# Gated delta-rule attention on one core: the carried part of the second tile scaled on GpSimd and summed in PSUM, both key-query products masked in one instruction, and a new order of issue

## The reference, cut to what matters

```python
decay = where(tril, exp(g[:, None] - g[None, :]), 0)
M = where(stril, (k_beta @ k.T) * decay, 0)
T = solve_triangular(eye + M, eye)
v_c, k_cumdecay = T @ v_beta, T @ (k_beta * exp(g)[..., None])
# over the chunks, with a state of 128x128:
v_new = v_i - k_cumdecay @ state
out = (q_i * exp(g_i)[:, None]) @ state + (q_i @ k_i.T * dec_i) @ v_new
state = state * exp(g_last) + (k_i * exp(g_last - g_i)[:, None]).T @ v_new
```

## Time and profile before

| what | value |
|---|---|
| median of three runs | 1482.04 us |
| the profiled execution | 1480.87 us |
| its span in the trace | 1479.0 us |
| granted TensorE clock over the span | 0.974 |
| PE / DVE / ACT / POOL busy, share of the span | 89% / 77% / 68% / 35% |
| rounds of the attention | 64, the first `w` 0 at 81.0 us, the last at 1143.1 us |

### The profile page before, as it was taken

The page is one execution under the profiler, slowest core; times in us unless marked ns, Lnnn a source line. Parts: engine busy times, 40 slices in busy tenths (PEclk is TensorE's granted clock), DMA queues, the critical chain, the costliest instruction groups (busy, mean ns, idle before and its releaser), DMA issues.

```text
span 1479.0 us, 34092 instructions
## 1 busy us (share of the span) xinstructions
PE 1309.4 (89%) x11516; PEld 927.9 (63%) x11516; DVE 1138.0 (77%) x2414; ACT 1002.5 (68%) x2170; POOL 517.4 (35%) x599
## 2 busy tenths in 40 slices
PE   2679999999999999999999999999987559999995
PEld 2247666766667676767667676766665436666664
DVE  4678978889898989888898989898866445555555
ACT  2579788897979798888979797988865212222221
POOL 0134242334334242433333342424323105555550
PEclk9999999999999999999999999999999859999998
DMA  2111010101011010101010110100001016444441
GB/s 82 41 39 52 9 51 9 52 9 58 14 47 44 16 52 9 51 9 52 9 58 27 33 45 16 52 23 16 23 15 33 1 36 182 150 150 152 157 153 39
DMA packets 44659, 76.37 MB, mean 52 GB/s; under 512 B 7172, under 2 KB 26022, under 8 KB 44488
## 3 DMA queue, kind: packets, MB, share of 16 engines
q1 hardware_dynamic: 44488, 74.19, 16.1%
HBM read 72.85 MB, written 1.32 MB: 50 GB/s over the span
## 4 chain that ended last, share of the span: by engine, by line
PE 70%; DVE 16%; issue 7%; ACT 5%; DMA 1%; DVEq 1%; SPq 1%; ACTq 0%
PE bank L563 13%; PE bank L517 9%; PE bank L780 8%; PE bank L733 6%; DVE sil L1132 5%; PE bank L710 5%; PE bank L606 4%; PE bank L724 3%; PE bank L618 3%; PE bank L582 3%; PE bank L646 2%; PE bank L638 2%; DVE t L1192 2%; PE bank L713 2%; PE bank L696 2%
## 5 line engine op out<-in xcount | busy, mean ns | idle before, releaser
L563 PE MATMUL bank<-xT,whl 128*128 128x512 f16 x1152 | 298.3, 383 | 18.1 <-DVE sil L1132 8.3
L1132 DVE SCALAR_TENSOR_TENSOR sil<-bank,cw,sil 128x510 f32<-128x510 f32 (+2 forms) x384 | 283.3, 738 | 7.1 <-ACT sil L855 4.5
L1393 POOL TENSOR_TENSOR nl<-nt,n 128x512 f16<-128x512 f32 x64 | 74.1, 1157 | 523.6 <-ACT n L939 523.6
L1192 DVE CAST_PREDICATED t<-levm,bank 128x256 f16<-128x256 uint8 x384 | 166.1, 433 | 90.4 <-PE bank L638 74.5
L1021 ACT ACTIVATE kq<-vtok 128x512 f16<-128x512 f32 x94 | 59.2, 630 | 192.1 <-DVE vtok L1323 192.1
L950 ACT ACTIVATE x<-bank 128x256 f16<-128x256 f32 x320 | 125.6, 393 | 69.7 <-PE bank L618 68.2
L1205 DVE CAST_PREDICATED u<-levm,bank 128x256 f16<-128x256 uint8 x384 | 162.9, 424 | 0.2
L1323 DVE SCALAR_TENSOR_TENSOR vtok<-bank,b1s,zs 128x512 f32<-128x512 f32 x94 | 70.6, 751 | 117.6 <-PE bank L517 117.6
L563 PEld LDWEIGHTS bank<-xT,whl 128*128 128x128 f16 x1152 | 97.2, 98 | 94.9 <-DVE sil L1132 12.7
L618 PEld LDWEIGHTS bank<-t,n 128*128 128x128 f16 x1536 | 84.4, 98 | 89.2 <-DVE t L1192 59.8
L517 PE MATMUL bank<-xT,wmhl 128*128 128x512 f16 x564 | 139.2, 384 | 0.0
(11 more groups left out here) (156 smaller groups left out, 3118.1 us busy)
## 6 DMA issues: line engine op xcount, KB each, us to landing
grow<-rowsc SPq DMA_DIRECT2D x64, 256.0 KB, 3.3
wt<-wqkvz SPq DMA_DIRECT2D x16, 768.0 KB, 4.5
wms<-wm SPq DMA_DIRECT2D x47, 256.0 KB, 4.0
zs<-gsc SPq DMA_DIRECT2D x18, 512.0 KB, 3.7
wo<-wout SPq DMA_DIRECT2D x16, 256.0 KB, 4.2
zs<-gsc SPq DMA_DIRECT2D x8, 448.0 KB, 3.8
zs<-gsc SPq DMA_DIRECT2D x8, 384.0 KB, 3.6
zs<-gsc SPq DMA_DIRECT2D x9, 320.0 KB, 3.6
```

The costliest lines, as they stand in the source:

```text
L563: mm = nc.tensor.matmul(dst[:, :], whl[:, h, k, col:col + HD], xT[:, l, k, half * 512:(half + 1) * 512], start=(k == 0 and m == 0), stop=( ...
L1132: nc.vector.scalar_tensor_tensor(out=dst[:, :, late:S], in0=src[:, :, 0:S - late], scalar=cw[:, q, i, 3 - late:4 - late], in1=dst[:, :, la ...
L1192: nc.vector.copy_predicated(halves(t16[:, pair(U)], n)[:, :, :, 0], by4(2 * n, n), packed(X_BANK, n)).then_inc(s_tup, 1)
```

## The change

`qx` becomes two instructions, one for each value head, each over 256 columns: it multiplies the key part of `cross` as well as the query part by exp(g) of the second tile. `p` takes the scaled key part as its left side, as two matmuls of 128 columns instead of one of 256, and waits for `qx` instead of `cross`. The per-token scalar is so gone from the right side: `r1h` is one instruction over both heads (`vtok` less `R_BANK`), and `r1` is gone, since `y1` 1 adds to what `p` left in `R_BANK` and `rr` 1 takes `vtok` less that sum. `KQ_BANK` and `KB_BANK` become the halves of one PSUM tensor, `kk` writes its third product with a gap so that both have one layout, and `mask` is one instruction of 512 columns. `cross` and the waits on `mask` follow. Four small tiles of the expert part are placed in `sil`. `SLOT` and `FRONT` are written anew.

```diff
...
         def sem(name):
             return ctx.enter_context(nc.semaphore(name))
-        bank = [ctx.enter_context(nc.psum_tensor(f"bank{i}", [P, 512], F32)) for i in range(8)]
+        bank = [ctx.enter_context(nc.psum_tensor(f"bank{i}", [P, 512], F32)) for i in range(2)]
+        products = ctx.enter_context(nc.psum_tensor("products", [P, 1024], F32))
+        KQ_BANK, KB_BANK = products[:, 0:512], products[:, 512:1024]
+        bank += [KQ_BANK, KB_BANK]
+        bank += [ctx.enter_context(nc.psum_tensor(f"bank{i}", [P, 512], F32)) for i in range(4, 8)]
         FB = bank[0:2]
-        KQ_BANK, KB_BANK = bank[2], bank[3]
         X_BANK, WT_BANK = bank[4], bank[5]
...
         at = sb("at", [P, 3, 2, 2, P])
-        qx = sb("qx", [P, 3, 2, P])
+        qx = sb("qx", [P, 3, 2, 2, P])
         n16 = sb("n16", [P, 3, 4, P], F16)
...
         rr = sb("rr", [P, 2, P], F16)
-        r1 = sb("r1", [P, 2, P])
         r1h = sb("r1h", [P, 2, P], F16)
...
         gb = zs[:].rearrange("p q v t -> p (q v) t")
-        lg = sb("lg", [P, NT, 34])
-        lrep = sb("lrep", [P, NT, 34])
+        late = sil[:, 3]
+        lg, lrep, gates = (late[:, n * NT * NE:(n + 1) * NT * NE].rearrange("p (t e) -> p t e", t=NT) for n in range(3))
         m8 = sb("m8", [P, NT, 8])
         red = sb("red", [P, NT])
-        gates = sb("gates", [P, NT, NE])
         gTs = wo[0:NE].rearrange("p q v n -> p (q v n)")
-        gT = sb("gT", [NE, TOK])
+        gT = sil[0:NE, 2]
         s_const, s_w, s_mconst, s_out = map(sem, ("s_const", "s_w", "s_mconst", "s_out"))
...
                 if unit_index(U) <= BEHIND:
-                    wait_u(pe, s_mask, (G, b - 1), 2, 2)
+                    wait_u(pe, s_mask, (G, b - 1), 1, 1)
                     wait_u(pe, s_cross, (G, b - 1), 1, 1)
...
                 wait_u(pe, s_acc, (G, b - BEHIND - 1), 1, 1)
-                nc.tensor.matmul(KB_BANK[:, 0:256], kq[:, q, b, 0, P:S], kq[:, q, b, :, P:S], start=True, stop=True
+                nc.tensor.matmul(KB_BANK.rearrange("p (k c i) -> p k c i", k=2, c=2)[:, :, 0], kq[:, q, b, 0, P:S], kq[:, q, b, :, P:S], start=True, stop=True
                                  ).then_inc(s_kk, 1)
...
                 else:
-                    wait_u(pe, s_r1h, U, 2, 2)
+                    wait_u(pe, s_r1h, U, 1, 1)
                     wait_u(pe, s_vn, U, 2, 1)
...
                     wait_u(pe, s_r, (G, b - 1), 2, 2)
-                else:
-                    wait_u(pe, s_r1, U, 2, 2)
                 guess = y0[:].rearrange("p v d -> p (v d)")
-                nc.tensor.matmul(R_BANK[:, 0:256], eye[:, 0], guess, start=True, stop=False, skip_group_check=True)
+                nc.tensor.matmul(R_BANK[:, 0:256], eye[:, 0], guess, start=(c == 0), stop=False, skip_group_check=True)
                 for v in range(2):
...
             def p(U, _):
-                wait_u(pe, s_cross, U, 1, 1)
+                wait_u(pe, s_qx, U, 2, 2)
                 wait_u(pe, s_v0s, U, 2, 2)
                 wait_u(pe, s_r, U, 2, 1)
-                nc.tensor.matmul(R_BANK[:, 0:256], cross[:, pair(U), 0], v0s[:, pair(U)].rearrange("p v d -> p (v d)"),
-                                 start=True, stop=True).then_inc(s_p, 1)
+                for v in range(2):
+                    mm = nc.tensor.matmul(R_BANK[:, v * P:(v + 1) * P], qx[:, third(U), v, 0], v0s[:, pair(U), v],
+                                          start=(v == 0), stop=False, skip_group_check=True)
+                mm.then_inc(s_p, 1)
             def o(U, _):
...
                 wait_u(pe, s_at, U, 2, 2)
-                wait_u(pe, s_qx, U, 1, 1)
+                wait_u(pe, s_qx, U, 2, 2)
                 if unit_index(U) + BEHIND < HQK * B:
-                    wait_u(pe, s_mask, (G, b + BEHIND), 2, 1)
+                    wait_u(pe, s_mask, (G, b + BEHIND), 1, 1)
                     wait_u(pe, s_cross, (G, b + BEHIND), 1, 1)
...
                         if c == 1:
-                            mm = nc.tensor.matmul(dst, v0s[:, pair(U), v], qx[:, third(U), v], start=False, stop=True,
+                            mm = nc.tensor.matmul(dst, v0s[:, pair(U), v], qx[:, third(U), v, 1], start=False, stop=True,
                                                   skip_group_check=True)
...
                 act.wait_ge(s_row[n % 2], 16 * (n // 2) + 16)
-                wait_u(act, s_qx, (G, b - 2), 1, 1)
+                wait_u(act, s_qx, (G, b - 2), 2, 2)
                 nc.scalar.activation(exb[:, w], grow[:, w, :, 1], ACT.Exp).then_inc(s_exb, 1)
...
             def cross_(U, _):
...
                 wait_u(act, s_kk, U, 2, 1)
-                wait_u(act, s_mask, U, 2, 1)
-                wait_u(act, s_p, (G, b - 2), 1, 1)
-                wait_u(act, s_qx, (G, b - 2), 1, 1)
+                wait_u(act, s_mask, U, 1, 1)
+                wait_u(act, s_qx, (G, b - 2), 2, 2)
                 nc.scalar.copy(cross[:, w], KQ_BANK[:, :].rearrange("p (k c i) -> p k c i", k=2, c=2)[:, :, 1]
...
                                         rs[:, i].rearrange("p (b s) -> p b s", b=B), ALU.mult).then_inc(s_kq, 1)
-            def mask(U, c):
+            def mask(U, _):
                 (G, b), w = U, pair(U)
...
                 wait_u(dve, s_nt, (G, b - 2), 1, 1)
-                wait_u(dve, s_kk, U, 2, c + 1)
-                if c == 0:
-                    src = KQ_BANK[:, :].rearrange("p (k c i) -> p k c i", k=2, c=2)[:, :, 0]
-                else:
-                    src = KB_BANK[:, 0:256].rearrange("p (k i) -> p k i", k=2)
-                nc.vector.tensor_tensor(kqm[:, w, c], src, mask2, ALU.mult).then_inc(s_mask, 1)
+                wait_u(dve, s_kk, U, 2, 2)
+                nc.vector.tensor_tensor(kqm[:, w], products[:, :].rearrange("p (c k h i) -> p c k h i", c=2, k=2, h=2)[:, :, :, 0],
+                                        mask2.unsqueeze(1).to_broadcast([P, 2, 2, P]), ALU.mult).then_inc(s_mask, 1)
             def decayed(U, _):
...
                 wait_u(dve, s_exp, U, 1, 1)
-                wait_u(dve, s_mask, U, 2, 2)
+                wait_u(dve, s_mask, U, 1, 1)
                 wait_u(dve, s_nl, (G, b - 2), 1, 1)
...
                     wait_u(dve, s_y, U, 4, 2)
-                    wait_u(dve, s_r1, U, 2, 2)
-                src = vtok[:, q, 2 * b] if c == 0 else r1[:]
-                nc.vector.tensor_tensor(rr[:], src, R_BANK[:, 0:256].rearrange("p (v d) -> p v d", v=2),
+                nc.vector.tensor_tensor(rr[:], vtok[:, q, 2 * b + c], R_BANK[:, 0:256].rearrange("p (v d) -> p v d", v=2),
                                         ALU.subtract).then_inc(s_r, 1)
-            def right_side(U, dst, ready):
+            def right_side(U, _):
                 (G, b), q = U, U[0][1] % 2
...
                 wait_u(dve, s_y, (G, b - 1), 4, 4)
-                wait_u(dve, s_r, (G, b - 1), 2, 2)
-                for v in range(2):
-                    nc.vector.scalar_tensor_tensor(
-                        out=dst[:, v], in0=R_BANK[:, v * P:(v + 1) * P],
-                        scalar=sc[:, q, C_NEG, v, 2 * b + 1:2 * b + 2],
-                        in1=vtok[:, q, 2 * b + 1, v], op0=ALU.mult, op1=ALU.add).then_inc(ready, 1)
-
-            def rounded_side(U, _):
-                right_side(U, r1h, s_r1h)
-
-            def exact_side(U, _):
-                right_side(U, r1, s_r1)
+                nc.vector.tensor_tensor(r1h[:], vtok[:, q, 2 * b + 1],
+                                        R_BANK[:, 0:256].rearrange("p (v d) -> p v d", v=2), ALU.subtract
+                                        ).then_inc(s_r1h, 1)
             def hz_(U, _):
...
             def attention_part(U, v):
...
                 wait_u(pool, s_exp, U, 1, 1)
-                wait_u(pool, s_mask, U, 2, 2)
+                wait_u(pool, s_mask, U, 1, 1)
                 wait_u(pool, s_o, (G, b - 3), 1, 1)
                 nc.gpsimd.tensor_tensor(at[:, third(U), v], kqm[:, w, :, 1], ex[:, w, v], ALU.mult).then_inc(s_at, 1)
-            def carried_part(U, _):
+            def carried_part(U, v):
                 (G, b), w = U, pair(U)
...
                 wait_u(pool, s_o, (G, b - 3), 1, 1)
-                nc.gpsimd.tensor_tensor(qx[:, third(U)], cross[:, w, 1:2].to_broadcast([P, 2, P]), exb[:, w], ALU.mult
-                                        ).then_inc(s_qx, 1)
+                nc.gpsimd.tensor_tensor(qx[:, third(U), v], cross[:, w], exb[:, w, v].unsqueeze(1).to_broadcast([P, 2, P]),
+                                        ALU.mult).then_inc(s_qx, 1)
             attention({"cw": scale_cw, "wo": scale_wo, "sq": square, "eye": start_inverse, "nl": low_n,
```

171 lines of the change are left out of this document (85 added, 86 removed), and 8 rows, old and new, of the table SLOT.

## The result

| what | before | after |
|---|---|---|
| median of six runs each, taken side by side | 1482.27 us (1478.9 to 1484.3) | 1474.06 us (1471.2 to 1474.9) |
| the profiled execution, and its span | 1480.87, 1479.0 | 1472.83, 1470.9 |
| granted TensorE clock over the span | 0.974 | 0.973 |

The ratio of the medians is 0.9943, with a 95% interval of 0.9928 to 0.9959: 8.2 us faster, where 17 were forecast. The sign was right and the time lies inside the range, but the gain is half of what was worked out, and it does not come from where the forecast had it.

The account below looks back on a forecast made before the run. No single engine was taken as the bound: DVE in the first two rounds, PE in the third. Rounds of 16.0, 16.1, 17.6 and 16.8 us gave 66.5 against 67.56 a group, 17 us over 16 groups: 1465 us, range 1436 to 1491.

Parts of the forecast that it names:

- DVE, -0.78 us a round: Masks and right sides in every round: 1.72 us of DVE work removed, 0.94 added, 3.1 us less a group.
- PE, zero: p as four records of 128 columns instead of two of 256: no PE cost, at most 0.2 us a round.
- GpSimd, covered by idle time: The added qx multiplication, 726 ns a round, 46.5 us in all, costs nothing because GpSimd has idle time.
- So in this trace GpSimd pays, and I charge DVE nothing: When GpSimd and DVE meet at SBUF, only GpSimd's copy lengthens (615 to 1668 ns); DVE's product stays 680 to 694.
- The order: New issue order moves work between rounds: PE 0, +0.65, -1.50, +0.85 us; with the edit, 66.5 us a group against 67.56.
- PE-bound, 19.14 - 1.50 = 17.6: Third round: moving fills out takes 1.50 us off PE and the round; ACT, 16.1 us busy, does not take over.
- Start and tail unchanged: Start and tail of the kernel keep their work; moving four small tiles costs nothing there.
- All groups look alike: Twelve middle groups of 67.57 us stand for all 16, so the 1.06 us gain a group gives 17 us.
- No difference, evened out and paid back: Rival: PE bound nearly everywhere, third round's -1.50 us paid back by +0.65 and +0.85 in second and fourth; 1482, chance 0.15.
- The late GpSimd: Rival: wo waits for its load in the second round, delaying at, eye and qx; 1502 at 3 us late, chance 0.14.
- The port: Rival: DVE's nt and hT wait for the added qx each round, 0.73 us x 64; 1512 at most, chance 0.03.
- More than that: Rival: DVE's 3.1 us a group come through whole, 64.5 us a group, 49 us gained, 1433; chance 0.15.

Follow-up runs that it names:

- right_side_only: Kernel before, old order and two masks, with only the new right side (qx twice, p over qx, r1h whole, r1 gone); 1489.76 us, ratio 1.0059.
- new_order_old_code: Code of the kernel before (two masks, r1h and r1, one qx) in the new order of issue; 1485.29 us, ratio 1.0041 to before.
- less_pe_third: Changed kernel with one matmul instead of three in rest 9 and rest 10, 0.86 us less PE work in the third round; 1468.32 us, ratio 0.9915 to before.
- more_dve: Changed kernel with one more DVE operation of 512 columns a round ahead of acc, into a spare tile; 1496.46 us, ratio 1.0120 to before.
- more_gpsimd_old: Kernel before with one more GpSimd product ahead of each qx, into an unused tile; 1485.93 us, ratio 1.0024.
- five_moves: Changed kernel with nmul 1, tap 16, evict 16, evict 17 and lo 1 issued later; 1535.66 us, ratio 1.0369 to before.

## Why the prediction was wrong

**DVE, -0.78 us a round: right as work, wrong as time.** The two new instructions cost what their nearest rows said, and DVE's busy time in the twelve groups is down by 32 us. But the right side's part lay beside `proj`, `xe` 3 and `w` 3 in the old order, and the one mask cost 0.99 us a group there and gives at most 0.13 in the new one. The premise that the first and second rounds are DVE-bound because DVE is busy 15.46 of 16.18 us was too strong: right_side_only takes 0.96 us of DVE records out of each round (four of 341 ns for one of 408) and no round gets shorter. In the new order the edit gives 0.28 and 0.44 us there.

**PE, zero:** right; `p` holds the chain for 0.53 us in after where it held it for 0.51, and new_order_old_code and after have the same rounds where PE is fullest (third 18.45 against 18.47, fourth 17.34 both).

**GpSimd, covered by idle time: wrong in the old order,** by 0.24 us a group, since the added work pushed `qx` into DVE's `hT`. In the new order its price was not measured by itself. "So in this trace GpSimd pays, and I charge DVE nothing" rested on the records of `nt` up to 1080 us; the `hT` of 1.28 us at 1080.62 is the other side of it in the same trace, and was overlooked. DVE's records do lengthen, `nt` from 685 to 882 ns, by the new order rather than the added work, though beside the chain in the third round, where they are longest.

**The order: the term that was mis-sized.** By round, forecast against measured (means of the twelve groups, against before): first -0.18 and -0.75; second +0.42 and +0.60; third -1.54 and -0.68; fourth +0.24 and +0.78. The failed step is the third round: "PE-bound, 19.14 - 1.50 = 17.6", with "ACT [...] does not take over". I passed on PE's whole -1.50 us because PE was busy 18.60 of 19.14. PE's busy time fell by 1.28, and the round by 0.68, to 18.47; the rest turned into idle time, of which the largest piece is the wait of `w` 5 for `xe` 5 on ACT, 0.95 us in after and nothing in before; ACT's busy time in the round fell by 1.0 where I had counted 1.9. less_pe_third gives a price measured in the new order, 0.37 us for one: 1.50 x 0.37 = 0.56, near the 0.68. The same too-kind reading stands in the fourth round, where I charged 0.2 to 0.3 for +0.85 of PE work because the round had that much idle time; the round took 0.78 of it. Added PE work did not fall into that idle time; the DVE work that more_dve adds in the third round did. On the other side the first round gained 0.57 us more than forecast: of its 0.75, the edit made 0.28 and the order 0.47, although a tap was added. I had priced the order there by its DVE work alone; which of its moves in that round gives the 0.47 was not tried. Together the four rounds come to -0.05 where -1.06 was forecast.

**Start and tail unchanged: right within a scatter of one or two us. "All groups look alike": wrong for the last two,** where all of the difference that holds is. I had read twelve groups in the middle and multiplied by 16. That 8.2 us came off at all is luck: nothing in the sum stands for the gain of the last two groups. The clock of 0.98 and 0.93 there was in the trace before and could have been read.

**The rivals.** "No difference, evened out and paid back" (0.15) is what the groups in the middle did, to 0.05 us, but not in the way it was told: the third round gave back 0.68 instead of 1.50, the second and fourth took 1.38, and the first round's 0.75 closed the account. The late GpSimd did not come: nothing in after waits for `eye` or `at`. The port (0.03 at 1512) is real, and its price where it was measured, in the old order, is 0.24 us a group, much smaller than its price at most. "More than that" fell with right_side_only.

## What to carry over

A round in which an engine is busy for 95% does not yet move one for one with that engine's work: here a us on PE was worth 0.37 us in the third round and a us on DVE anything from nothing to 0.75 us by round, and one run that removes or adds a us gives that rate before a schedule is judged by differences of work. Merging two instructions can cost the earlier one's start, as the mask did: look at who waits for the first of the two. Cut the trace at its ends as well as in its middle, since the stretches that don't repeat can hold all of the gain.

## What was not expected of the hardware

GpSimd and DVE hold each other up in both directions. The prediction had seen only GpSimd's copy stretch, to 1668 ns. With GpSimd's work moved or added, DVE's `hT` took 1.03 us in the second rounds and up to 1.30 in more_gpsimd_old instead of 0.68, and `nt` up to 1.28 in after. The path paid 0.24 us a group for it in more_gpsimd_old.

TensorE's granted clock fell to 0.50 for about the length of one `kk` in rounds that otherwise kept 1.00, and doubled that `kk`, 1.38 to 2.72 us; in five_moves the same followed a wait that a single late DVE step had made. The executions of the kernel before also differ among themselves with the clock: 1474.92 us at a mean of 0.978, 1484.06 at 0.970. Which part of the execution falls, and why in one and not in the other, stays open.
